# Attention: the first batch is weighed ahead of the second one's transposes, with two projections between those and its weighing

## What is computed

```python
x = rmsnorm(hidden_states, ln1_w)
q = einsum('bsh,dh->bsd', x, q_w).reshape(b, s, NH, QHD)[..., :NOPE]    # NH = 16 heads of 128
k, v = ...                                                            # the same from kv_w
scores = einsum('bqnd,bknd->bnqk', q, k) * scale                       # 4 x 16 of 256 x 256
p = softmax(where(causal, scores, -1e9))
attn = einsum('bnqk,bknd->bqnd', p, v)
attn_out = einsum('bsd,hd->bsh', attn.reshape(b, s, NH * VD), o_w)
```

## Time and profile before

| | |
|---|---|
| median of 3 runs | 778.53 us (777.67 to 779.28) |
| profiled execution | 778.94 us |
| its span, first to last instruction | 776.8 us |
| granted TensorE clock, mean | 0.990 |
| TensorE busy | 734.0 us (94%) |
| VectorE busy | 568.2 us (73%) |
| ScalarE busy | 458.3 us (59%) |
| GpSimd busy | 347.6 us (45%) |

### The profile page before, as it was taken

One profiled execution on the slowest core, in us unless ns is written; L12 is line 12 of the kernel. 1 busy time (PEld: TensorE's weight loads), 2 busy tenths in 40 slices (PEclk: granted clock), 3 DMA queues, 4 the chain that ended last, 5 costly groups with the idle time before them and its releaser, 6 DMA issues.

```text
span 776.8 us, 12318 instructions
## 1 busy us (share of the span) xinstructions
PE 734.0 (94%) x4036; PEld 572.8 (74%) x4036; DVE 568.2 (73%) x1218; ACT 458.3 (59%) x1022; POOL 347.6 (45%) x309
## 2 busy tenths in 40 slices
PE   7996899999989999999999999998998999999996
PEld 3443455455545888998989889887777888888986
DVE  3689999998898678847775785676675565647376
ACT  4699868868674467627664674576662433425153
POOL 1007989998779644404332342224433221313130
PEclk9998999999999999999999999999999999999999
DMA  8022433443231100100100100001228161515101
GB/s 324 16 75 82 115 102 102 129 105 102 74 86 68 55 28 28 44 12 29 55 28 0 54 27 28 22 22 62 83 79 237 59 178 49 146 51 181 47 0 54
DMA packets 25212, 59.02 MB, mean 76 GB/s; under 512 B 3616, under 2 KB 5152, under 8 KB 25040
## 3 DMA queue, kind: packets, MB, share of 16 engines
q1 hardware_dynamic: 25024, 58.21, 25.1%
q10 hardware_dynamic: 144, 0.26, 0.1%
HBM read 57.21 MB, written 1.25 MB: 75 GB/s over the span
## 4 chain that ended last, share of the span: by engine, by line
PE 49%; issue 18%; DVE 14%; POOL 11%; ACT 6%; DMA 1%; SPq 0%; DVEq 0%; POOLq 0%; ACTq 0%
PE ps L1036 10%; PE ps L1038 9%; PE ps L1037 9%; PE ps L551 8%; POOL a_p L1163 4%; POOL m_ring L408 3%; PE ps L500 3%; DVE m_ring L905 3%; POOL a_wl L1157 2%; PE ps L456 2%; PE ps L509 2%; PE ps L555 2%; DVE e_aw L2044 2%; PE ps L1222 1%; DVE e_sg L2036 1%
## 5 line engine op out<-in xcount | busy, mean ns | idle before, releaser
L1163 POOL TENSOR_TENSOR a_p<-a_p,a_rs 128x128 f32<-128x128 f32 (+1 forms) x128 | 61.4, 506 | 170.8 <-DVE a_rs L1481 170.8
L1705 POOL TENSOR_TENSOR e_wl<-raw,e_wh 128x512 fp32r<-128x512 f32 (+1 forms) x55 | 59.1, 1085 | 154.6 <-ACT e_wh L1841 86.3
L551 PE MATMUL ps<-m_ring,ident 128*128 128x512 f32 x256 | 120.6, 599 | 5.5 <-POOL m_ring L408 5.4
L408 POOL TENSOR_TENSOR m_ring<-m_ring,m_c_sb 128x1024 f32<-128x1024 f32 x40 | 95.0, 2387 | 15.2 <-DVE m_ring L905 13.7
L400 POOL TENSOR_TENSOR m_ring<-m_du,m_b_sb 128x1024 f32<-128x1024 f32 x31 | 74.1, 2391 | 59.8 <-DVE m_ring L892 59.8
L551 PEld LDWEIGHTS ps<-m_ring,ident 128*128 128x128 f32 x256 | 46.8, 190 | 49.7 <-issue 37.0
L1376 ACT ACTIVATE a_p<-a_p,a_nmax 128x128 f32<-128x128 f32 (+1 forms) x128 | 57.1, 447 | 37.3 <-DVE a_nmax L1474 37.0
L1036 PE MATMUL ps<-a_rowsh,e_wh 128*128 128x512 f32 x200 | 78.3, 391 | 0.2 <-ACT e_sg L1886 0.2
L1037 PE MATMUL ps<-a_rowsl,e_wh 128*128 128x512 f32 x200 | 77.9, 389 | 0.0
L1038 PE MATMUL ps<-a_rowsh,e_wl 128*128 128x512 f32 x200 | 77.8, 389 | 0.0
L905 DVE TENSOR_TENSOR_SCAN m_ring<-m_first,ps 128x1024 f32<-128x1024 f32 x32 | 72.8, 2275 | 6.7 <-ACT ps L754 4.5
(11 more groups left out here) (232 smaller groups left out, 2116.3 us busy)
## 6 DMA issues: line engine op xcount, KB each, us to landing
raw<-in_expert_w SPq DMA_DIRECT2D x30, 384.0 KB, 3.5
raw<-in_attn_w SPq DMA_DIRECT2D x20, 512.0 KB, 3.3
m_c_sb<-bc SPq DMA_DIRECT2D x40, 256.0 KB, 3.4
m_b_sb<-bc SPq DMA_DIRECT2D x32, 256.0 KB, 4.1
e_wb<-wt SPq DMA_DIRECT2D x18, 256.0 KB, 4.7
e_wb<-wt SPq DMA_DIRECT2D x4, 448.0 KB, 5.3
e_wb<-wt SPq DMA_DIRECT2D x4, 384.0 KB, 4.3
x<-in_x_tok SPq DMA_DIRECT2D x1, 1024.0 KB, 9.6
```

The source lines that it names most:

```text
L408: nc.gpsimd.tensor_tensor(split(slot(n)), split(slot(n)), c_sb[:, k % C_BUFS:k % C_BUFS + 1, :].to_broadcast([P, 2, HALF]), ALU.mult).then ...
L551: nc.tensor.matmul(ps[:, Y_BANK + c, :], ident[:, :], slot(n)[:, c * HALF:(c + 1) * HALF], start=False, stop=False, skip_group_check=True) ...
L1163: nc.gpsimd.tensor_tensor(p[:, b, cols], p[:, b, cols], rs[:, b, t:t + 1].to_broadcast([P, count]), ALU.mult).then_inc(norm_done, 1)
L1705: nc.gpsimd.tensor_tensor(w[1][:, k, cols], raw[:, k, cols], w[0][:, k, cols].bitcast(F32), ALU.subtract).then_inc(low, 1)
```

## The change

Three lists are edited, in each head but (3, 3). On TensorE `weigh` of batch 0 (the first of the four) goes ahead of `turn` of the second batch, and `fill(3)` goes up ahead of `weigh` of the second batch, so that `fill(2)` and `fill(3)` stand between that turn and its weighing. On ScalarE `high_o` of the first batch goes ahead of `high_p` and `exps`, and the high part of projection 3 ahead of `high_o` of the second batch and of `pack`. On VectorE `low_o` of the first batch goes ahead of `low_p` of the second and of two `one_over`, and the low part of projection 3 ahead of `low_o` of the second. GpSimd's and SyncE's lists stay as they are.

```diff
--- before.py
+++ after.py
@@ -1325,11 +1325,11 @@
             turn(n, 0)
             fill(1)
             scores(n + 3, j, 3)
+            weigh(n, j, 0)
             turn(n + 1, 1)
-            weigh(n, j, 0)
             fill(2)
+            fill(3)
             weigh(n + 1, j, 1)
-            fill(3)
             turn(n + 2, 2)
             turn(n + 3, 3)
             fill(4)
@@ -1421,13 +1421,13 @@
             high_p(n, 0)
             exps(n + 2, 2)
             fill(1)
+            high_o(n, j, 0)
             high_p(n + 1, 1)
             exps(n + 3, 3)
-            high_o(n, j, 0)
             fill(2)
+            fill(3)
             high_o(n + 1, j, 1)
             pack(j, g * 16 + 32, OUT_COLS if isinstance(g, int) and g == NG - 1 else slice(0, PACK))
-            fill(3)
             high_p(n + 2, 2)
             high_p(n + 3, 3)
             fill(4)
@@ -1552,13 +1552,13 @@
             low_p(n, 0)
             fill(1)
             maxes(n + 3, 3)
+            low_o(n, j, 0)
             low_p(n + 1, 1)
             one_over(n + 2, 2)
             one_over(n + 3, 3)
-            low_o(n, j, 0)
             fill(2)
+            fill(3)
             low_o(n + 1, j, 1)
-            fill(3)
             low_p(n + 2, 2)
             low_p(n + 3, 3)
             fill(4)
```

## The result

| | kernel before | changed kernel |
|---|---|---|
| median, 9 runs each | 778.53 us (777.38 to 783.33) | 784.88 us (782.89 to 786.31) |
| ratio | | 1.0075, 95% interval 1.0059 to 1.0091 |
| profiled execution / span | 778.94 / 776.8 us | 784.48 / 782.6 us |
| mean granted TensorE clock | 0.990 | 0.989 |

The change makes the kernel 0.75% slower, about 5.8 us by the ratio (the two medians differ by 6.35 us, inside the ratio's interval of 4.6 to 7.1 us). The forecast was 783.4 (+4.9), with a range of 780.5 to 786.5.

What follows compares the result with a forecast made beforehand. TensorE, busy 94% of the span, was taken as the bound, with each head clocked by projection 4's end. Fourteen full heads at 0.35 us add 4.9 to 778.5, giving 783.4 us, 8-in-10 range 780.5 to 786.5.

Steps and rivals of the forecast that it cites:

- TensorE's own order: TensorE, turn 1 to turn 2: the reordered weighings and projections end at the same time, 397.09, so 0 cost.
- VectorE, 0.66 us: VectorE: the low_o moved ahead holds the engine 0.66 us, making one_over(n + 2, 2) that much later.
- Turn 3, 0.40 of wait and 0.35 of delay: TensorE's turn 3 waits 0.40 us for GpSimd's batch 3; projection 4 starts 0.35 us late per head.
- ScalarE, the second lag beside the first: ScalarE: high_p(n + 2) stands behind pack, making weigh 2 0.43 us late; it runs beside turn 3's lag, not added.
- rival (b): Turn 3 does not wait, pack alone delays 12 heads by 0.34: 4.1 us, 782.6; chance 0.70 together with the forecast.
- No swallowing at turn 0: TensorE's 0.41 us wait at the next head's turn 0 cannot absorb projection 4's delay, as both ends move.
- The sum: Whole attention: 14 full heads x 0.35 = 4.9 us slower; head (3, 2) about 0, head (3, 3) not edited.
- (a): Nothing measurable changes because turn 3's slack holds: 778.5 us; chance 0.09.
- (c): The two lags add, 14 x 0.35 + 12 x 0.43 = 10.1 us: 788.6; chance 0.07 shared with the drain.
- (d): Faster: the chain from projection 4 to the next turn 0 shortens, at most 7 us, 771.5; chance 0.06.

Runs made afterwards that it cites:

- both lags removed: Changed kernel with VectorE's low_o(n, j, 0) back behind the two one_over and ScalarE's pack ahead of projection 3's high half, TensorE's order kept: 779.46 us, ratio 0.9994.
- pack early: Changed kernel with ScalarE's pack moved up between the high halves of projections 2 and 3, VectorE staying changed: 784.56 us, ratio 1.0059 to the kernel before.
- the tail with one edit: Kernel before with VectorE's one_over(n + 4, 0) ahead of low_o(n + 3, j, 3) instead of behind it: 777.82 us, ratio 0.9995.

## Why the prediction was right

- **TensorE's own order, 0.** Right: turn 2 starts at 397.09 by the clock of the earlier trace rows, as foretold, and with both lags removed the time is that of before (0.9994, +0.4 us in the profile).
- **VectorE, 0.66 us.** 0.65 us measured. The Trainium skill ("VectorE: DVE Perf Modes", "The DRAIN you can't avoid"), by which the pair would hold the engine about 0.87 (an estimate from its figure), is not borne out by these rows if one takes that figure alone. The same section of the Trainium skill adds that a next instruction which isn't held starts earlier, and the prediction left that out: `low_p` starts at 398.92, before the second of the pair ends (398.72 and 0.29).
- **Turn 3, 0.40 of wait and 0.35 of delay.** The wait shows as 0.36, the delay as 0.34 in head (1, 3) and 0.37 on average.
- **ScalarE, the second lag beside the first.** Right in both parts: weigh 2 at 403.53 less 3.89 = 399.64 against 399.62 foretold; alone it costs 0.35 a head in the 12 heads of groups 0 to 2 and nothing in group 3. That was rival (b), 4.1 us, and two kernels measured 4.2 and 4.3 in the attention.
- **No swallowing at turn 0.** Right: the wait of the weight loader there goes only from 0.41 to 0.32 us, and the period still grows by 0.36. The 0.09 that is gone fits the 0.08 by which weigh 2 is later than projection 4 and which the prediction put into this slack.
- **The sum.** 14 x 0.35 = 4.9; the profile has 5.15 for the same heads and 0.07 for head (3, 2). What the sum lacks is head (3, 3), taken as untouched: 1.16 us at TensorE's lower clock, 1.24 in the second profile of the changed kernel. That term was missing, not mis-sized. The time came out inside the range all the same (784.88) because the term is small, which is luck and not part of the working.
- **Rivals.** (a) needed the slack of 0.26 us to hold, and it did not; (c) is excluded by 6.4 us instead of 10.1; (d) needed projection 4 earlier than before, and it is later.

What stays open is why the clock falls in four of fourteen profiles (the changed kernel twice, pack early, and the tail with one edit) and not in the others, which have sparse stretches like it. What it costs is plain in all fourteen: from the first to the last group of normalizations in head (3, 3) it is 5.09 to 5.33 us in the four profiles with a fall and 3.87 to 4.10 in the ten without. The order of group 3 takes part in where the waits lie, but no run isolates a condition.

## What to carry to other kernels

When an instruction moves forward in an in-order queue, everything it overtakes is late by its whole slot; list every reader of those results, on every engine, with its slack, because covering one (weigh 1, by a projection) leaves the next (GpSimd, then turn 3). Two lags of like size can hide each other, so undoing one shows little: undo them one at a time and together. And find what starts the next round: here it was a chain over three engines, and the gain lay in its order, where two moved lines gave 0.7%, not on the busiest engine.

## What was not expected of the hardware

The granted clock of TensorE fell for about 3.4 us near the end of the attention, behind a stretch in which it had been busy 5.0 of 7.6 us, in some kernels and not in others with as sparse a stretch. Single transposes took up to 421 instead of about 272 ns and the part cost 1.2 us, nearly a quarter of what the 14 heads cost. The Trainium skill ("TensorE: Matmul & The Clock Gate", "What's actually happening") has the gate throttled by default and released by activity; the fall behind sparse work agrees with that, but why the clock stayed at 1.00 behind work as sparse, no run here shows. Its lower level is 0.50, as the changed kernel's second profile has it from 539 to 541 us.
